# Pair attention of a one-core transformer tower: exponentials over three PSUM banks, two units in flight, a ring of six steps

## The chip, the cores and the metric

The kernel runs on one core of a Trainium2 chip. Times are device microseconds (us) of one execution. PE is TensorE, DVE is VectorE, ACT is ScalarE, POOL is GpSimd, SP is SyncE. Before: a median of 1665.47 us over 3 runs (1663.53 to 1667.87).

## What is computed

The whole is a tower of eight layers on a state h of 2 batches x 1025 tokens x 64 channels. The change touches one of them, the causal attention of 32 heads that are two channels wide:

```python
def _L2_attn_ref(x, w_qkv, w_proj, qn_w, kn_w):
    B, T, C = x.shape
    HD = 2
    H = C // HD
    qkv = x @ w_qkv.T
    q, k, v = jnp.split(qkv, 3, axis=-1)
    heads = lambda t: t.reshape(B, T, H, HD).transpose(0, 2, 1, 3)
    q = _rmsnorm(heads(q), qn_w)
    k = _rmsnorm(heads(k), kn_w)
    v = heads(v)
    scale = np.float32(1.0 / np.sqrt(HD))
    att = jnp.einsum('bhtd,bhsd->bhts', q, k) * scale
    causal = jnp.tril(jnp.ones((T, T), bool))
    att = jnp.where(causal, att, jnp.float32(-1e30))
    att = jax.nn.softmax(att, axis=-1)
    y = jnp.einsum('bhts,bhsd->bhtd', att, v)
    y = y.transpose(0, 2, 1, 3).reshape(B, T, C)
    return y @ w_proj.T
h = h + _L2_attn_ref(_layernorm(h, axis=-1), L2_attn_w_qkv, L2_attn_w_proj, L2_attn_qn_w, L2_attn_kn_w)
```

For each of 64 pairs of batch and head the kernel takes the exponential of half of a 1024 x 1024 matrix of scores, and the last token apart.

## The kernel before

`program` runs nine stages one after the other, each in blocks that end with a barrier of all engines; `stage_pairs` (L1937) is the sixth. It calls `pairs_prepare` (norms, projections), `pairs_attend` (L2113, the function that the change touches) and `pairs_project`.

`pairs_attend` works on four heads of one batch at a time, 16 such groups (`BH`). A group is cut into nine **steps** (the list `steps`). A step is one block of 128 keys against 512 queries, or two blocks whose queries together make 512: steps 1 and 8 are blocks of 384 and 128 queries, step 2 of 256 and 256. N = 144 steps in all, numbered n; s = n % 9 is the place in the group. A step goes through the engines so:

- **Scores** (PE, L2325): for each of the four heads q a matmul of 12 rows (bf16) x 512 queries into one PSUM bank, the four on rows 0, 32, 64 and 96 of the array. Two heads make a **unit** u, two banks; units use banks 0-1, 2-3, 4-5 in turn, so three are in flight. The first matmul of unit u waits until the exponential of unit u - 3 is done (`exp_ok`, u - 2 of them). The second signals `s_ps`.
- **Exponential** (ACT, L2255): one instruction of 128 x 1024 for each unit, 288 in all, from PSUM into the ring `PT` of RING = 4 steps. It waits for `s_ps`, and from step 4 on at every step for the weighing of step n - 3 (`av_ps`).
- **Mask** (DVE, L2239): for the steps in `diag` (0, 1, 2, 7, 8 of a group) a product with `keep`, 128 x 512, once or (steps 1, 2, 8) twice. It waits for both exponentials of its step.
- **Weighing** (PE, `weigh`, L2291, called by `attend`): weights times values in float32, four heads on the four column groups of the array, accumulated in bank 6. Half 0 of the queries ends with step 2, half 1 with step 8; DVE then copies bank 6 into `Yc` (L2232), and the next half waits for that copy (`y_sb`). The second block of step 2 is weighed with step 3, so step 2 has 256 columns, step 3 has 512 + 256.
- **Turns** (`TURNS`, PE L2280 and L2271 by way of bank 7, brought out by DVE at L2197 or L2185/L2187): after steps 0 to 3 of a group two transposes of the next group's q and two of its k, after steps 4 to 6 the results `Yc` of the group before.

What fixes the order is PE's own program, written out in the loop over n: the scores of step n, the weighing of step n - 2, the turn of step n. Every engine takes its instructions in that order and waits at the head of its queue. DVE's loop at step n is: the copy of bank 6 if the weighing of n - 2 ended a half, the turn, the mask of step n.

```python
for n in range(N + per):
    ...
        attend(n - 2)
    for t in turns_at(n):
        turn(*t)
```

Of the kernel before, what the change touches and what calls it, by code (L numbers as in the profile page):

```python
# [14 lines left out]
ACT = mybir.ActivationFunctionType  # L15
# [2097 lines left out]
def pairs_attend(nc, K, A, Q12, K12, V1, qk, Yt, YL):  # L2113


    SCALE = float(np.float32(1.0 / np.sqrt(2)))
# [6 lines left out]
    steps += [[(1, 5, 0, 128, 384), (1, 7, 384, 384, 128)]]  # L2123
    per = len(steps)
    diag = {0: (0,), 1: (0, 384), 2: (0, 256), 7: (0,), 8: (0, 384)}
    RING = 4
    N = BH * per

    TURNS = {0: ("q", 0), 1: ("q", 1), 2: ("k", 0), 3: ("k", 1), 4: ("y", 0), 5: ("y", 1), 6: ("y", 2)}
# [17 lines left out]
    masked = [0]  # L2147
    for n in range(N):
        masked.append(masked[-1] + (n % per in diag))
    with ExitStack() as ctx:  # L2150
        sb = lambda n, s, dt=F32: K.sb("pt_" + n, s, dt, ctx=ctx)
        sem = lambda n: K.sem("pt_" + n)
        ps = K.ps
# [1 line left out]
        keep = sb("keep", [128, 128])  # L2155
        QT = sb("QT", [128, 2, 1024], BF16)
        KT = sb("KT", [128, 2, 1024], BF16)
        PT = sb("PT", [128, RING, 4, 512])
        Yc = sb("Yc", [128, 2, 1024])
        rec = sb("rec", [128, 3, 4])  # L2160
        LP = sb("LP", [128, 2, 9, 96])
# [6 lines left out]
        with nc.Block() as block:  # L2168
# [4 lines left out]
            @block.vector  # L2173
            def _(dve):
                link = Chain(dve, chain)
                tt = nc.vector.tensor_tensor
                nc.vector.tensor_copy(identb[:], K.ident[:]).then_inc(id_ok, 1)

                def bring(bh, which, i):
                    dve.wait_ge(turn_ps, number[bh, which, i] + 1)  # L2180
                    if which == "y":
                        t0, t1 = YTILES[i]
                        y = ps[:, 7, 0:128 * (t1 - t0)].rearrange("p (t h e) -> p t h e", h=4, e=32)
                        r = rec[:, 0:t1 - t0]
                        link(nc.vector.reciprocal(r, y[:, :, :, 2]))  # L2185
                        g = 4 * (bh % 8)
                        ins = tt(Yt[:, (bh // 8) * 8 + t0:(bh // 8) * 8 + t1, g:g + 4], y[:, :, :, 0:2],  # L2187
                                 r.unsqueeze(3).to_broadcast([128, t1 - t0, 4, 2]), ALU.mult)
                    elif which == "last":
                        y = ps[0:1, 7, 0:192].rearrange("p (b h e) -> p b h e", b=2, e=3)  # L2190
                        link(nc.vector.reciprocal(LR[:], y[:, :, :, 2]))
                        ins = tt(YL[:], y[:, :, :, 0:2], LR[:].unsqueeze(3).to_broadcast([1, 2, 32, 2]), ALU.mult)
                    else:
                        if bh >= 2:
                            dve.wait_ge(s_ps, 2 * per * (bh - 1))
                        dst = QT if which == "q" else KT
                        ins = nc.vector.tensor_copy(dst[:, bh % 2, 512 * i:512 * i + 512],  # L2197
                                                    ps[:, 7, :].bitcast(BF16)[:, 0:512])
                    ins.then_inc(turn_sb, 1)

                def last_scores(b):
                    q = qk[:, 16 + b, 0:64]
                    kk = LP[:, b, :, 0:64]
                    link(tt(kk[:, 0:8], qk[:, 8 * b:8 * b + 8, 64:128], bc(q, 8), ALU.mult))
                    link(tt(kk[:, 8], qk[:, 16 + b, 64:128], q, ALU.mult))
                    ins = nc.vector.tensor_reduce(LS[:, b], kk.rearrange("p t (h e) -> p t h e", e=2), AX.X, ALU.add)
                    ins.then_inc(ls_ok, 1)

                def last_weights(b):
                    if b == 0:  # L2210
                        dve.wait_ge(le_ok, 1)
                        link(nc.vector.tensor_scalar(LS[:, :, 8], LS[:, :, 8], K.ident[:, 0:1], None, ALU.mult))
                    w = LP[:, b].rearrange("p t (h e) -> p t h e", e=3)
                    v = V1[:, 8 * b:8 * b + 8, 0:96].rearrange("p t (h e) -> p t h e", e=3)
                    link(tt(w[:, 0:8], v, LS[:, b, 0:8].unsqueeze(3).to_broadcast([128, 8, 32, 3]), ALU.mult))
                    link(tt(w[:, 8], V1[:, 16 + b, 0:96].rearrange("p (h e) -> p h e", e=3), bcl(LS[:, b, 8], 3),
                            ALU.mult))
                    nc.vector.tensor_reduce(LW[:, b], LP[:, b].rearrange("p t c -> p c t"), AX.X,
                                            ALU.add).then_inc(lw_ok, 1)

                for t in FIRST:
                    bring(*t)
                dve.wait_ge(c_in, 16)
                for n in range(N + per):
                    bh, s = n // per, n % per
                    if n >= 2 and n - 2 < N and (n - 2) % per in (2, 8):
                        c = (n - 2) % per // 8
                        k = 2 * ((n - 2) // per) + c
                        dve.wait_ge(av_ps, n - 1)
                        if k >= 4:  # L2230
                            dve.wait_ge(turn_ps, number[k // 2 - 2, "y", 2] + 1)
                        nc.vector.tensor_copy(Yc[:, k // 2 % 2, 512 * c:512 * c + 512], ps[:, 6, :]).then_inc(y_sb, 1)  # L2232
                    for t in turns_at(n):
                        bring(*t)
                    if n < N and s in diag:
                        dve.wait_ge(exp_ok, 2 * n + 2)
                        for c0 in diag[s]:
                            d = PT[:, n % RING, :, c0:c0 + 128]
                            ins = tt(d, d, bc(keep[:], 4), ALU.mult)  # L2239
                        ins.then_inc(mask_ok, 1)  # L2240
                    if s == 5 and bh in (1, 2):
                        last_scores(bh - 1)
                    if s == 5 and bh in (3, 4):
                        last_weights(bh - 3)

            @block.scalar
            def _(act):
                for n in range(N):
                    if n >= 4:
                        act.wait_ge(av_ps, n - 2)  # L2250
                    for i in range(2):
                        u = 2 * n + i
                        act.wait_ge(s_ps, u + 1)
                        b0 = 2 * (u % 3)
                        nc.scalar.activation(PT[:, n % RING, 2 * i:2 * i + 2, :], ps[:, b0:b0 + 2, :], ACT.Exp,  # L2255
                                             scale=SCALE).then_inc(exp_ok, 1)
                    if n == 3 * per:
                        act.wait_ge(ls_ok, 2)
                        nc.scalar.activation(LS[:], LS[:], ACT.Exp, scale=SCALE).then_inc(le_ok, 1)

            @block.tensor
            def _(pe):
# [23 lines left out]
                def weigh(n, parts, start, stop):  # L2286
                    bh = n // per
                    for k, (c, j, p0, q0, w) in enumerate(parts):
                        for q in range(4):
                            v0 = 3 * (4 * (bh % 8) + q)  # L2290
                            ins = nc.tensor.matmul(ps[32 * q:32 * q + 32, 6, q0:q0 + w],  # L2291
                                                   V1[:, (bh // 8) * 8 + j, v0:v0 + 32],
                                                   PT[:, n % RING, q, p0:p0 + w], start=start and k == 0,
                                                   stop=stop and k == len(parts) - 1, skip_group_check=True)
                    return ins

                def attend(n):
                    bh, s = n // per, n % per
                    pe.wait_ge(exp_ok, 2 * n + 2)
                    if s in diag:  # L2300
                        pe.wait_ge(mask_ok, masked[n + 1])
                    if s in (0, 3) and n:
# [12 lines left out]
                for n in range(N + per):  # L2315
                    bh, s = n // per, n % per
                    if n < N:
                        if s == 0:
                            pe.wait_ge(turn_sb, number[bh, "k", 1] + 1)
                        for q in range(4):  # L2320
                            u = 2 * n + q // 2
                            if q % 2 == 0 and u >= 3:
                                pe.wait_ge(exp_ok, u - 2)
                            for c, j, p0, q0, w in steps[s]:
                                ins = nc.tensor.matmul(ps[:, 2 * (u % 3) + q % 2, p0:p0 + w],  # L2325
                                                       KT[32 * q:32 * q + 12, bh % 2, j * 128:(j + 1) * 128],
                                                       QT[32 * q:32 * q + 12, bh % 2, c * 512 + q0:c * 512 + q0 + w],
                                                       start=True, stop=True)
                            if q % 2:
                                ins.then_inc(s_ps, 1)  # L2330
                    if 2 <= n < N + 2:
                        attend(n - 2)
# [718 lines left out]
```

## Time and profile before

| | |
|---|---|
| median of 3 runs | 1665.47 us |
| profiled execution, its own time | 1676.74 us |
| its span on the core | 1675.0 us |
| busy: PE, DVE, ACT, POOL | 1342.4, 1018.7, 861.0, 367.5 us |
| TensorE clock granted, share of full speed, whole span | 0.83 |
| `pairs_attend`: first exponential starts, last ends | 786.7 us, 1055.3 us |
| exponentials of the stage (L2255) | 288, 266.1 us busy |

Busy shares are of the whole span and average over stages; the stage in question is some 270 us of it, and what bounds it is to be read from a stretch within it. A waiting instruction is named with what released it. Matmuls overlap one another: a row that says "x8 ... 1.07" is eight matmuls from the start of the first to the end of the last, and PE can start the next kind before that end.

### The profile page before, as it was taken

The numbers are of one execution on the slowest core, as the hardware profiler recorded it, in microseconds if no ns is written. First come the engines' busy times: TensorE is split into PE (matmuls) and PEld (weight loads), VectorE is DVE, ScalarE is ACT, GpSimd is POOL, SyncE is SP. The second block draws the span as 40 slices with busy tenths as digits, with TensorE's granted clock in tenths as the row PEclk, the third lists the DMA queues.
The fourth block names the chain that finished last, engine by engine and source line by source line (L and its number), as shares of the span: only waits on it lengthen the run. The fifth ranks groups of instructions, "written<-read, shape, count | busy, mean of one in ns | idle before, by whom it ended". The sixth has DMA issues, their size and how long they took to land. (4 is left out here: it accounts for less than half of the span.)

```text
span 1675.0 us, 28770 instructions
## 1 busy us (share of the span) xinstructions
PE 1342.4 (80%) x11573; PEld 780.8 (47%) x11573; DVE 1018.7 (61%) x1983; ACT 861.0 (51%) x1716; POOL 367.5 (22%) x409
## 2 busy tenths in 40 slices
PE   6658993975488929973999999686899999977995
PEld 3547982775434425541333333444454445554342
DVE  0467556845794185657574545425799999964233
ACT  1330222121304723346999999321799999952121
POOL 0002400000051200000000000000599999940000
PEclk9865996555656959985999999767699999996898
DMA  6000000013000000000000000001000000001000
GB/s 124 8 12 10 1 2 8 1 22 49 11 1 1 1 14 1 1 2 2 1 2 1 2 1 2 10 0 23 9 2 2 2 2 2 2 5 25 1 1 13
DMA packets 37692, 15.87 MB, mean 9 GB/s; under 512 B 33588, under 2 KB 36798, under 8 KB 37296
## 3 DMA queue, kind: packets, MB, share of 16 engines
q1 hardware_dynamic: 37560, 14.04, 4.1%
q8 instruction: 92, 1.51, 0.4%
q14 instruction: 40, 0.33, 0.1%
HBM read 12.98 MB, written 1.05 MB: 8 GB/s over the span
## 5 line engine op out<-in xcount | busy, mean ns | idle before, releaser
L2910 POOL TENSOR_SCALAR da_AD<-di_QH,di_KH 128x256 f32<-128x256 f32 x320 | 287.5, 926 | 52.8 <-POOLq L2689 47.4
L2895 ACT ACTIVATE da_AD<-ps,di_NK 128x256 f32<-128x256 f32 x760 | 288.3, 840 | 0.5
L2871 DVE TENSOR_TENSOR da_AD<-ps,di_KH 128x1024 f32<-128x1024 f32 x240 | 273.4, 1216 | 0.9
L2255 ACT ACTIVATE pt_PT<-ps 128x1024 f32<-128x1024 f32 x288 | 266.1, 1103 | 6.3 <-PE ps L2325 6.0
L2946 PE MATMUL ps<-da_AD,da_win 128*32 128x256 f32 x4080 | 241.7, 384 | 19.6 <-ACT da_AD L2895 14.6
L2946 PEld LDWEIGHTS ps<-da_AD,da_win 128*32 128x32 f32 x4080 | 123.0, 110 | 133.9 <-ACT da_AD L2895 39.5
L2291 PE MATMUL ps<-pt_PT,pa_V 128*32 128x512 f32 (+3 forms) x1536 | 155.5, 499 | 8.3 <-DVE pt_Yc L2232 3.2
L2239 DVE TENSOR_TENSOR pt_PT<-pt_PT,pt_keep 128x512 f32<-128x512 f32 x128 | 84.2, 689 | 61.2 <-ACT pt_PT L2255 60.1
L2325 PE MATMUL ps<-pt_QT,pt_KT 12*128 12x512 bf16 (+3 forms) x768 | 80.1, 334 | 3.2 <-DVE pt_KT L2197 0.5
L2623 PE MATMUL ps<-cp_XT,cp_W 96*128 96x342 f32 x192 | 75.1, 518 | 0.0
L2568 ACT ACTIVATE cp_H<-ps 128x342 f32<-128x342 f32 x48 | 21.9, 457 | 102.8 <-PE ps L2623 102.8
L2449 POOL MEMSET sw_xo<- 114x576 f32 x1 | 0.6, 578 | 330.3 <-POOLq L151 330.3
L1923 PE MATMUL ps<-mt_X,ew_wp 128*128 128x342 bf16 (+1 forms) x396 | 70.2, 314 | 1.3 <-ACT mt_WT L1854 0.8
L2291 PEld LDWEIGHTS ps<-pt_PT,pa_V 128*32 128x32 f32 x1536 | 38.9, 109 | 64.8 <-issue 63.6
L2535 DVE TENSOR_SCALAR cp_H<-ps 128x342 f32<-128x342 f32 x48 | 24.2, 513 | 72.5 <-PE ps L2623 72.4
L1868 ACT ACTIVATE mt_act<-ps 128x342 f32<-128x342 f32 (+1 forms) x66 | 30.1, 456 | 69.5 <-PE ps L1925 66.1
L662 ACT COPY rc_T<-ps 114x228 f32<-114x228 f32 x54 | 18.9, 349 | 81.7 <-PE ps L609 81.7
L1835 DVE TENSOR_TENSOR mt_prod<-ps,mt_act 128x342 f32<-128x342 f32 (+1 forms) x66 | 33.9, 514 | 37.3 <-ACT mt_act L1868 37.3
L2623 PEld LDWEIGHTS ps<-cp_XT,cp_W 96*128 96x128 f32 x192 | 35.8, 207 | 36.7 <-issue 28.4
L1582 PE MATMUL ps<-gq_KT,gq_QT 96*114 96x342 bf16 (+2 forms) x144 | 44.1, 433 | 10.7 <-DVE gm_mx L1511 8.6
L1923 PEld LDWEIGHTS ps<-mt_X,ew_wp 128*128 128x128 bf16 (+1 forms) x396 | 36.2, 101 | 34.6 <-DVE mt_H L1836 14.3
L654 DVE TENSOR_TENSOR rc_XX<-ps,rc_XX 114x456 f32<-114x456 f32 (+1 forms) x54 | 32.1, 594 | 32.1 <-PE ps L623 32.1
(721 smaller groups left out, 2391.3 us busy)
## 6 DMA issues: line engine op xcount, KB each, us to landing
em_xs<-in_x_dram SPq DMA_DIRECT2D x2, 1152.0 KB, 14.0
em_xs<-in_x_dram SPq DMA_DIRECT2D x2, 1024.0 KB, 18.2
ew_win<-in_L_ffn_w_dram SPq DMA_DIRECT2D x4, 320.0 KB
cp_W<-in_L_ffn_w_dram SPq DMA_DIRECT2D x2, 512.0 KB
em_WS<-in_L_tok_W_dram SPq DMA_DIRECT2D x8, 72.0 KB
la_blk<-la_scratch SPq DMA_DIRECT2D x8, 64.1 KB
dp_tokrow<-in_c_tokenrow_dram SPq DMA_DIRECT2D x1, 513.0 KB
la_scratch<-la_q SPq DMA_DIRECT2D x1, 512.0 KB
```

The lines of the kernel that those rows point to most:

```text
L1582: ins = nc.tensor.matmul(ps[0:P, b0 + c, 0:w], QT[0:96, h, t * P:(t + 1) * P], KT[0:96, h // 2, k0:k0 + w], start=True, stop=True)
L1835: link(tt(prod[0:r, n % 2], ps[0:r, b0 + 1, 0:GRP], act_sb[0:r, n % 2], ALU.mult))
L1923: nc.tensor.matmul(ps[0:r, b0 + i, 0:GRP], wp[:, k, i, 128 * c:128 * c + r], x_[:, cols], start=(k == 0), stop=(k == 2))
L2239: ins = tt(d, d, bc(keep[:], 4), ALU.mult)
L2255: nc.scalar.activation(PT[:, n % RING, 2 * i:2 * i + 2, :], ps[:, b0:b0 + 2, :], ACT.Exp, scale=SCALE).then_inc(exp_ok, 1)
L2291: ins = nc.tensor.matmul(ps[32 * q:32 * q + 32, 6, q0:q0 + w], V1[:, (bh // 8) * 8 + j, v0:v0 + 32], PT[:, n % RING, q, p0:p0 + w], start= ...
L2325: ins = nc.tensor.matmul(ps[:, 2 * (u % 3) + q % 2, p0:p0 + w], KT[32 * q:32 * q + 12, bh % 2, j * 128:(j + 1) * 128], QT[32 * q:32 * q + ...
L2623: nc.tensor.matmul(ps[:, n % 4, 0:GRP], W1[:, c * 128:(c + 1) * 128], XT[:, g * GRP:(g + 1) * GRP], start=True, stop=True).then_inc(up_ps, 1)
L2871: nc.vector.tensor_tensor(AD[:, n % RING], bc(QD[:, u % 2], 4), bcl(kk, SELP), ALU.max).then_inc(ad_dve, 1)
L2895: ins = nc.scalar.activation(AD[:, n % RING, q], QA[:, u % 2], ACT.Abs, bias=NK[:, u, s:s + 1])
L2910: ins = nc.gpsimd.tensor_scalar(AD[:, n % RING, q], QH[:, u], KH[:, u, s:s + 1], None, ALU.max)
L2946: ins = nc.tensor.matmul(ps[32 * q:32 * q + 32, e % 4, 0:SELP], w, AD[:, n % RING, q], start=False, stop=last, skip_group_check=True)
```

## The change

`WIDE` = 3 heads make a unit instead of two. A unit is three consecutive score banks of the stream m = 4n + q, so that a unit crosses steps: in three steps (12 heads) lie four units, [q0 q1 q2], [q3 | q0 q1], [q2 q3 | q0], [q1 q2 q3]. Units use banks 0-2 and 3-5 in turn, so two are in flight: the first matmul of unit u waits for the exponential of unit u - 2. The exponential is one instruction of 128 x 1536, 192 in all. The ring of weights `PT` becomes 24 slots, six steps. Masks and weighings of step n wait for `units(n)`, the last unit that holds a head of step n.

```diff
-    RING = 4
+    RING = 6
+    WIDE = 3
+    SLOTS = 4 * RING
...
+    def units(n):
+        return (4 * n + 3) // WIDE + 1
...
-        PT = sb("PT", [128, RING, 4, 512])
+        PT = sb("PT", [128, SLOTS, 512])
...
-                        dve.wait_ge(exp_ok, 2 * n + 2)
+                        dve.wait_ge(exp_ok, units(n))
...
-                for n in range(N):
-                    if n >= 4:
-                        act.wait_ge(av_ps, n - 2)
-                    for i in range(2):
-                        u = 2 * n + i
-                        act.wait_ge(s_ps, u + 1)
-                        b0 = 2 * (u % 3)
-                        nc.scalar.activation(PT[:, n % RING, 2 * i:2 * i + 2, :], ps[:, b0:b0 + 2, :], ACT.Exp,
-                                             scale=SCALE).then_inc(exp_ok, 1)
+                for u in range(4 * N // WIDE):
+                    last = WIDE * u + WIDE - 1
+                    if last >= SLOTS:
+                        act.wait_ge(av_ps, (last - SLOTS) // 4 + 2)
+                    act.wait_ge(s_ps, u + 1)
+                    b0, p0 = WIDE * (u % 2), WIDE * u % SLOTS
+                    nc.scalar.activation(PT[:, p0:p0 + WIDE, :], ps[:, b0:b0 + WIDE, :], ACT.Exp,
+                                         scale=SCALE).then_inc(exp_ok, 1)
...
                         for q in range(4):
-                            u = 2 * n + q // 2
-                            if q % 2 == 0 and u >= 3:
-                                pe.wait_ge(exp_ok, u - 2)
+                            m = 4 * n + q
+                            if m % WIDE == 0 and m >= 2 * WIDE:
+                                pe.wait_ge(exp_ok, m // WIDE - 1)
...
-                                ins = nc.tensor.matmul(ps[:, 2 * (u % 3) + q % 2, p0:p0 + w],
+                                ins = nc.tensor.matmul(ps[:, m % (2 * WIDE), p0:p0 + w],
...
-                            if q % 2:
+                            if m % WIDE == WIDE - 1:
                                 ins.then_inc(s_ps, 1)
```

The matmuls of PE keep their order; what moves is where it waits for an exponential, and after which matmul it signals one. The lists below give PE's instructions with the semaphores waited for. The program reuses semaphores of earlier stages, so they have those names: `md_hid_sb` is `exp_ok`, `md_y_ps` is `mask_ok`, `md_row_sb` is `turn_sb`, `la_c_in` is `y_sb`, `md_y_sb` is `av_ps`. L2325 is the scores (L2330 after the change), L2291 (L2296) the weighing, L2271 (L2276) and L2280 (L2285) turns.

**PE, steps 6 and 7 of the second group, before.**

```order
L2325 MATMUL ps<-pt_QT,pt_KT 128x512 [waits md_hid_sb]
L2325 MATMUL ps<-pt_QT,pt_KT 128x512
L2325 MATMUL ps<-pt_QT,pt_KT 128x512 [waits md_hid_sb]
L2325 MATMUL ps<-pt_QT,pt_KT 128x512
L2291 MATMUL ps<-pt_PT,pa_V 32x512 [waits md_hid_sb]
L2291 MATMUL ps<-pt_PT,pa_V 32x512 x3
L2271 MATMUL ps<-ident,pt_Yc 128x128 [waits la_c_in,md_row_sb]
L2271 MATMUL ps<-ident,pt_Yc 128x128
L2325 MATMUL ps<-pt_QT,pt_KT 128x512 [waits md_hid_sb]
L2325 MATMUL ps<-pt_QT,pt_KT 128x512
L2325 MATMUL ps<-pt_QT,pt_KT 128x512 [waits md_hid_sb]
L2325 MATMUL ps<-pt_QT,pt_KT 128x512
```

**The same place after the change.**

```order
L2330 MATMUL ps<-pt_QT,pt_KT 128x512 [waits md_hid_sb]
L2330 MATMUL ps<-pt_QT,pt_KT 128x512 x2
L2330 MATMUL ps<-pt_QT,pt_KT 128x512 [waits md_hid_sb]
L2296 MATMUL ps<-pt_PT,pa_V 32x512 [waits md_hid_sb]
L2296 MATMUL ps<-pt_PT,pa_V 32x512 x3
L2276 MATMUL ps<-ident,pt_Yc 128x128 [waits la_c_in,md_row_sb]
L2276 MATMUL ps<-ident,pt_Yc 128x128
L2330 MATMUL ps<-pt_QT,pt_KT 128x512 x2
L2330 MATMUL ps<-pt_QT,pt_KT 128x512 [waits md_hid_sb]
L2330 MATMUL ps<-pt_QT,pt_KT 128x512
L2296 MATMUL ps<-pt_PT,pa_V 32x512 [waits md_hid_sb]
```

Before, a unit's two score matmuls stand side by side. After, the unit that begins with the second wait has its first matmul ahead of the weighing and the turn, and its other two behind them; the next one has two ahead of a weighing and one behind.

**PE, steps 0 and 1 of the third group, before.**

```order
L2325 MATMUL ps<-pt_QT,pt_KT 128x512 [waits md_hid_sb,md_row_sb]
L2325 MATMUL ps<-pt_QT,pt_KT 128x512
L2325 MATMUL ps<-pt_QT,pt_KT 128x512 [waits md_hid_sb]
L2325 MATMUL ps<-pt_QT,pt_KT 128x512
L2291 MATMUL ps<-pt_PT,pa_V 32x512 [waits md_y_ps,md_hid_sb]
L2291 MATMUL ps<-pt_PT,pa_V 32x512 x3
L2280 MATMUL ps<-pt_identb,pa_Q 128x128 [waits md_row_sb]
L2280 MATMUL ps<-pt_identb,pa_Q 128x128 x3
L2325 MATMUL ps<-pt_QT,pt_KT 128x384 [waits md_hid_sb]
```

**The same place after the change.**

```order
L2330 MATMUL ps<-pt_QT,pt_KT 128x512 [waits md_hid_sb,md_row_sb]
L2330 MATMUL ps<-pt_QT,pt_KT 128x512 x2
L2330 MATMUL ps<-pt_QT,pt_KT 128x512 [waits md_hid_sb]
L2296 MATMUL ps<-pt_PT,pa_V 32x512 [waits md_y_ps,md_hid_sb]
L2296 MATMUL ps<-pt_PT,pa_V 32x512 x3
L2285 MATMUL ps<-pt_identb,pa_Q 128x128 [waits md_row_sb]
L2285 MATMUL ps<-pt_identb,pa_Q 128x128 x3
L2330 MATMUL ps<-pt_QT,pt_KT 128x384
L2330 MATMUL ps<-pt_QT,pt_KT 128x128
L2330 MATMUL ps<-pt_QT,pt_KT 128x384
L2330 MATMUL ps<-pt_QT,pt_KT 128x128
L2330 MATMUL ps<-pt_QT,pt_KT 128x384 [waits md_hid_sb]
```

Here the weighing and a turn of four transposes have come between the first matmul of the second unit and its other heads.

**DVE, steps 0 and 1 of a group, after the change (the order of before, with other line numbers).** L2203 brings a turn out, L2245 is the mask, L2238 the copy of bank 6; `md_row_ps` is `turn_ps`, `md_hid_ps` is `s_ps`.

```order
L2203 COPY pt_QT<-ps 128x512 [waits md_hid_ps,md_row_ps]
L2245 TENSOR_TENSOR pt_PT<-pt_PT,pt_keep 128x4x128 [waits md_hid_sb]
L2238 COPY pt_Yc<-ps 128x512 [waits md_row_ps,md_y_sb]
L2203 COPY pt_QT<-ps 128x512 [waits md_hid_ps,md_row_ps]
L2245 TENSOR_TENSOR pt_PT<-pt_PT,pt_keep 128x4x128 [waits md_hid_sb]
L2245 TENSOR_TENSOR pt_PT<-pt_PT,pt_keep 128x4x128
```

The mask of step 0 stands ahead of the copy of bank 6 (step 8 of the group before). That order is not new; what the mask waits for is: the unit that also holds two heads of step 1.

## Rows read from the trace of the kernel before

**Rows 1.** Busy time in stretches: start:end, length, busy (x count) of each engine, granted clock, DMA.

```profile
core 0: us, PE busy (x) PEld busy (x) DVE busy (x) ACT busy (x) POOL busy (x), PEclk, DMA share, GB/s
786.00:796.00 10.00, 9.73 (x72) 3.15 (x76) 4.75 (x10) 7.54 (x8) 0.00 (x0) 0.52 0.01 2
796.00:1061.00 265.00, 252.44 (x2606) 85.72 (x2602) 149.34 (x323) 258.93 (x281) 0.00 (x0) 1.00 0.01 1
...
277.00:402.00 125.00, 102.02 (x412) 88.52 (x413) 70.49 (x178) 26.57 (x51) 2.51 (x5) 0.50 0.08 12
536.00:590.00 54.00, 46.72 (x406) 21.65 (x402) 9.12 (x22) 37.20 (x64) 12.86 (x31) 1.00 0.03 7
```

**Rows 2.** Groups of ACT by form: busy us, mean ns of one, idle before.

```profile
L2895 ACT ACTIVATE da_AD<-ps,di_NK 128x256 f32<-128x256 f32 x760 | 288.3, 840 | 0.5
L2255 ACT ACTIVATE pt_PT<-ps 128x1024 f32<-128x1024 f32 x288 | 266.1, 1103 | 6.3 <-PE ps L2325 6.0
L1665 ACT ACTIVATE gt_PT<-ps 114x684 f32<-114x684 f32 x48 | 32.8, 738 | 10.6 <-PE ps L1706 10.3
...
L1665 ACT ACTIVATE gt_PT<-ps 114x228 f32<-114x228 f32 x12 | 3.7, 359 | 2.9 <-PE ps L1706 2.9
```

**Rows 3.** The exponential's line alone: duration min/median/max in ns, first and last start.

```profile
L2255 ACT ACTIVATE pt_PT<-ps x288: 1017/1105/1217, 786.7 to 1054.2; 128x1024 f32<-128x1024 f32 x144
```

**Rows 4.** PE in order of time, 896 to 909 us: start, us, what.

```profile
895.99 0.64 PE L2291 MATMUL ps<-pt_PT,pa_V 128*32 128x256 f32 x8
896.57 0.55 PE L2271 MATMUL ps<-ident,pt_Yc 128*128 128x128 f32 x3
...
897.05 0.67 PE L2325 MATMUL ps<-pt_QT,pt_KT 12*128 12x512 bf16 x4
897.64 1.50 PE L2291 MATMUL ps<-pt_PT,pa_V 128*32 128x512 f32 x16
899.07 0.55 PE L2271 MATMUL ps<-ident,pt_Yc 128*128 128x128 f32 x3
899.55 0.40 PE L2325 MATMUL ps<-pt_QT,pt_KT 12*128 12x512 bf16 x4
899.88 1.07 PE L2291 MATMUL ps<-pt_PT,pa_V 128*32 128x512 f32 x8
900.88 0.44 PE L2271 MATMUL ps<-ident,pt_Yc 128*128 128x128 f32 x2
901.25 0.39 PE L2325 MATMUL ps<-pt_QT,pt_KT 12*128 12x512 bf16 x4
901.57 1.07 PE L2291 MATMUL ps<-pt_PT,pa_V 128*32 128x512 f32 x8
902.57 0.78 PE L2325 MATMUL ps<-pt_QT,pt_KT 12*128 12x384 bf16 x8
...
907.12 1.07 PE L2291 MATMUL ps<-pt_PT,pa_V 128*32 128x384 f32 x16
908.12 0.40 PE L2280 MATMUL ps<-pt_identb,pa_Q 128*128 128x128 bf16 x4
908.45 0.41 PE L2325 MATMUL ps<-pt_QT,pt_KT 12*128 12x256 bf16 x8
```

**Rows 5.** ACT by windows around 900 us; PEld's load released by an exponential's end.

```profile
894.28 2.99 ACT L2255 ACTIVATE pt_PT<-ps 128x1024 f32<-128x1024 f32 x3
...
894.28 5.74 ACT L2255 ACTIVATE pt_PT<-ps 128x1024 f32<-128x1024 f32 x6
...
897.32 0.09 PEld L2325 LDWEIGHTS ps<-pt_QT,pt_KT 12*128 12x128 bf16 x2 [0.19 <-ACT pt_PT L2255]
898.82 7.75 ACT L2255 ACTIVATE pt_PT<-ps 128x1024 f32<-128x1024 f32 x8
900.04 1.02 ACT L2255 ACTIVATE pt_PT<-ps 128x1024 f32<-128x1024 f32 x1
```

**Rows 6.** DVE masks and copies of bank 6 by form; between them, a weighing after a copy.

```profile
L2239 DVE TENSOR_TENSOR pt_PT<-pt_PT,pt_keep 128x512 f32<-128x512 f32 x128 | 84.2, 689 | 61.2 <-ACT pt_PT L2255 60.1
...
909.08 0.64 PE L2291 MATMUL ps<-pt_PT,pa_V 128*32 128x512 f32 x4 [0.23 <-DVE pt_Yc L2232]
L2232 DVE COPY pt_Yc<-ps 128x512 f32<-128x512 f32 x32 | 22.1, 692 | 10.4 <-PE ps L2291 9.7
```

**Rows 7.** Waits in 786 to 1058 us: us in total, times, longest.

```profile
PEld ps L2325 <- ACT pt_PT L2255: 35.3, 89, 0.8
...
ACT pt_PT L2255 <- PE ps L2325: 6.0, 3, 4.2
```

**Rows 8.** PE at the stage's start, at the lower clock.

```profile
790.19 1.94 PE L2291 MATMUL ps<-pt_PT,pa_V 128*32 128x512 f32 x8
792.05 0.61 PE L2280 MATMUL ps<-pt_identb,pa_K 128*128 128x128 bf16 x4
792.60 0.61 PE L2325 MATMUL ps<-pt_QT,pt_KT 12*128 12x512 bf16 x4
```

More of the change, by code:

```diff
@@ L2194, in bring @@
                         if bh >= 2:
-                            dve.wait_ge(s_ps, 2 * per * (bh - 1))
+                            dve.wait_ge(s_ps, 4 * per * (bh - 1) // WIDE)
                         dst = QT if which == "q" else KT
@@ L2235, in _ @@
                     if n < N and s in diag:
-                        dve.wait_ge(exp_ok, 2 * n + 2)
+                        dve.wait_ge(exp_ok, units(n))
                         for c0 in diag[s]:
-                            d = PT[:, n % RING, :, c0:c0 + 128]
+                            d = PT[:, 4 * n % SLOTS:4 * n % SLOTS + 4, c0:c0 + 128]
                             ins = tt(d, d, bc(keep[:], 4), ALU.mult)
@@ L2247, in _ @@
             def _(act):
-                for n in range(N):
-                    if n >= 4:
-                        act.wait_ge(av_ps, n - 2)
-                    for i in range(2):
-                        u = 2 * n + i
-                        act.wait_ge(s_ps, u + 1)
-                        b0 = 2 * (u % 3)
-                        nc.scalar.activation(PT[:, n % RING, 2 * i:2 * i + 2, :], ps[:, b0:b0 + 2, :], ACT.Exp,
-                                             scale=SCALE).then_inc(exp_ok, 1)
-                    if n == 3 * per:
+                for u in range(4 * N // WIDE):
[6 more added lines that the diff above has]
+                                         scale=SCALE).then_inc(exp_ok, 1)
+                    if u == 3 * 4 * per // WIDE:
                         act.wait_ge(ls_ok, 2)
@@ L2292, in weigh @@
                                                    V1[:, (bh // 8) * 8 + j, v0:v0 + 32],
-                                                   PT[:, n % RING, q, p0:p0 + w], start=start and k == 0,
+                                                   PT[:, (4 * n + q) % SLOTS, p0:p0 + w], start=start and k == 0,
                                                    stop=stop and k == len(parts) - 1, skip_group_check=True)
@@ L2298, in attend @@
                     bh, s = n // per, n % per
-                    pe.wait_ge(exp_ok, 2 * n + 2)
+                    pe.wait_ge(exp_ok, units(n))
                     if s in diag:
```

## The prediction

> **What bounds the kernel now.** I read the busy time in stretches first. The change lies in one stage, which starts at 786 us. In its steady part ACT is busy 258.93 us of 265, and the clock granted to PE is 1.00 [rows 1]. Next the groups: ACT's part is 288 exponentials, 266.1 us busy with 6.3 us idle [rows 2]. So ACT sets the stage's time: 266.1 / 16 = 16.63 us for each group of four heads (18 exponentials of 0.924). The waits agree: PE waited 89 times for an exponential, ACT only 3 times for scores [rows 7].
>
> PE in order of time shows how near it comes [rows 4]. I take the distance from the start of one kind to the start of the next: scores 0.33 (899.55 to 899.88), weighing of 512 columns 1.00 (901.57 to 902.57), of 384 + 128 also 1.00 (907.12 to 908.12), of 256 0.58 (895.99 to 896.57), of 512 + 256 1.43 (897.64 to 899.07), turn of three 0.48, of two 0.37, of q or k 0.33 (908.12 to 908.45). A group has nine scores (2.97), weighings of nine times 512 columns (9.0) and seven turns (2.65): 14.6, some 15 with the scores in two pieces. PE has 1.6 us to spare in 16.6.
>
> The same rows show what happens when a long piece of PE lies between an exponential's end and the next scores. The exponentials from 894.28 end at 897.27; PE loads weights at 897.32 [rows 5] and from 897.33 does the last two scores of a step, the long weighing, a turn of three, and at 899.55 new scores, which end at 899.95 [rows 4]. ACT starts on them at 900.04. In a stream it starts one every 0.91 (898.82 is the sixth from 894.28), so it was due at 899.73 [rows 5]. ACT has lost 0.31 us there, with three units in flight; as exponentials overlap, only 0.02 of it show as idle. From it I take three delays: exponential's end to scores 0.06, scores' start to their end 0.40, that to ACT's start 0.09 (0.49 together).
>
> **What the change costs, part by part.** *The exponential of 1536.* Alone, 228 columns take 359 ns, 684 take 738 and 1024 take 1017 [rows 2, 3]: 0.83 ns a column. So 1536 take L = 1.44 us alone. In a stream 1024 start every 0.91 us; 0.42 more makes E = 1.33. Lower bound: the 256-wide ones take 288.3 / 760 = 0.379 each in a stream, against 0.924, or 0.71 ns a column: E = 1.29, L = 1.38. I take the first, from exponentials of the same kind. Twelve units a group by 1.33 are 15.97 against 16.63: ACT needs 0.66 less, 10.5 us in the stage. That is the whole gain there is, if ACT never waits. The Trainium skill, "ScalarE: Activation LUTs", section "What ACT_TABLE_LOAD costs", gives 186 ns + 0.833 ns a column, with 93 ns of overlap back to back; by it the 96 instructions removed would be worth 96 x 93 ns = 8.9 us, an estimate. The rows give 18 x 0.907 less 15.97, or 0.06 for each of the six removed in a group, and the 0.31 on top.
>
> *Two units in flight, cut across the steps.* A unit may be written once the unit two before it is done. Two of four units have a weighing in the middle. Let ACT start unit U3 of the last cycle at T, with its end at T + 1.44, and take weighings w1, w2 and turns t1, t2. U0 starts at T + 1.33. PE writes the first bank of U1 at T + 1.50 (0.33), weighs w1, turns t1, writes two banks (0.49): U1 starts at T + 2.32 + w1 + t1 (T + 3.32 + t1 for a weighing of 1.00), where ACT was free at T + 2.66. For U2 PE goes on: 0.33, w2, t2, one bank and 0.49. U2 starts at T + 2.65 + w1 + w2 + t1 + t2, or 1.33 after U1. U3 and the next U0 are whole, and follow by 1.33 each if nothing else is late. Three steps so take 5.98 + t1 + t2, against 5.44 of ACT before.
>
> Through a group, measured from the start of its U0:
> - Steps 0 to 2: U1 after 2.33 (t1 = 0.33), U2 after 1.75 (t2 = 0.33, pieces of 384 and 128 about 0.1), U3 after 1.33. The next U0 is late by DVE: the mask of step 0 now waits for U1's end (0.05, 0.69), the copy of bank 6 stands behind it (0.69) and the weighing of step 0 waits for that copy [rows 6]; then 1.00, a turn 0.33, scores 0.49. U0 starts 1.44 + 3.31 after U1: at 7.08.
> - Steps 3 to 5: mask of step 1 and turn let U1 come 1.97 later, then 1.37 (weighing 0.58, turn 0.48), 1.33, and 1.51 for U0, behind the weighing of 1.43 and a turn of 0.48: 6.19.
> - Steps 6 to 8: 2.16 (turn 0.37), 1.36, 1.33, 1.33: 6.18.
>
> Sum 19.45 us against 16.63: 2.82 a group, 45.1 in 16. The first group has no results to turn nor copy to wait for, about 1 less: **+44 us**. The lower clock at the start (0.52 for 10 us [rows 1]) is there in both, and may cost up to 2 more where PE is now in the path.
>
> *Ring of six.* ACT's wait for a weighing moves from three steps back to five. I cost it at nothing: the 0.31 before 900.04 is explained by scores that ended at 899.95, while the weighing ended at 899.14 (897.64 + 1.50) [rows 4]. Masks and weighings are the same in number. The masks' 84.2 us of DVE lie beside; what they hold up is counted above.
>
> **The sum.** The profiled execution took 1676.74 us, 11.3 above the median; nothing in the stage explains that, so I carry the difference over: 1720.7 for it, 1665.47 + 44 = **1709.5** for the median. Bounds: with E = 1.29 and L = 1.38, 0.27 less a group, 1705. Exponentials in a stream last longer, up to 1217 ns with a median of 1105 [rows 3]; 0.09 more of L enters about four times a group, and gives 1715. Twelve distances of PE and DVE a group, each good to 0.05, are 10 us either way. Own range 1698 to 1722.
>
> **Rivals.**
> - *The change works: PE always has three banks ready, ACT is the bound.* 15.97 a group, 1665.5 - 10.5 = **1655**. For it: PE busy for 15 of 16. It needs w1 + t1 under 0.34, where U1 is no longer late (T + 2.32 + w1 + t1 against T + 2.66); the weighing alone is 1.00 [rows 4], and the same reckoning gives 900.04 for the late exponential of before. 0.07.
> - *Half of the stalls vanish,* in distances that overlap where I add them: each group 1.4 less or more so, down to no change at **1665**: 0.03.
> - *PE's clock falls.* PE is now idle in many short waits; 15 of 19.45 us is 77% of the time. The trace has both: a stretch at 1.00 with PE busy 46.72 of 54, and one at 0.50 with 102.02 of 125 [rows 1]. At the lower level a weighing of 512 takes 1.86 (790.19 to 792.05) and a turn 0.55 [rows 8]: nine weighings 16.7, seven turns 3.9, nine scores at about a turn 5.0, together 25.6, over 6 us a group more. In half of the stage that is 50 us, **1759**; from the first fall it decides. The Trainium skill, "TensorE: Matmul & The Clock Gate", section "A second HAM failure mode: psum-queue depth-cycling", says that a PE which idles briefly again and again while it cycles through PSUM banks swings between its two clocks. By that page the later time would come; no stretch of this stage shows it so far, at 95% busy. 0.09.
>
> **How the numbers follow.** My forecast has 0.81. A measurement of this kernel can tell about 0.3% (5 us) from no change. Faster by more: only the first rival, 0.07. Same: 0.03. Slower: forecast and clock, 0.90. The range needs 8 in 10: nine tenths of the forecast's 0.81 in its own range, and a little more on both sides for stalls partly absorbed and for a clock that falls a short while: 1694 to 1728.
>
> **What would show it.** Exponentials: 192, of about 1.44 to 1.5 us each. From the first one's start to the last one's, 267.4 us before, some 311. ACT idle before them, released by the scores: 16 x (19.45 - 15.97) = 56 us, in gaps up to 1.0 (the largest at steps 0 to 1, then 7 and 4). PE waits less for exponentials than it does now and still is in ACT's path. Clock 1.00 after the first 10 us. If gaps are there only where a turn lies inside the unit, the turns and not the weighings decide; if ACT's idle is under 15 us, the forecast is wrong and the first rival right; if the weighings' distances grow to 1.86, it is the clock; a mean far from 1.44 means the exponential was mis-sized.

## The result, and the profile after

The changed kernel takes 1732.76 us (median of 4 runs, 1723.87 to 1737.02), against 1664.50 for the kernel before (4 runs, 1657.42 to 1667.87): a ratio of 1.0413, 95% interval 1.0366 to 1.0459. It is slower, as forecast, by 68 us and not by 44, and outside the range.

One profile below, that with two full-array matmuls, is of a disturbed execution (1759.32 us) and is read for this stage alone; the medians given are of all runs of a kernel, the ratios leave such executions out.

The first figures to compare are those of ACT. Groups of the stage by form, as [rows 2], of the changed kernel:

```profile
L2260 ACT ACTIVATE pt_PT<-ps 128x1536 f32<-128x1536 f32 x192 | 268.7, 1452 | 81.5 <-PE ps L2330 80.8
L2296 PE MATMUL ps<-pt_PT,pa_V 128*32 128x512 f32 x768 | 118.2, 691 | 9.3 <-DVE pt_Yc L2238 7.7 <-DVE pt_PT L2245 1.2
```

The exponentials are 96 fewer and ACT is as busy as before, 268.7 us (rows now count each alone, since few overlap). Its idle time has gone from 6.3 to 81.5 us, and the scores end nearly all of it. The line alone, as [rows 3]:

```profile
L2260 ACT ACTIVATE pt_PT<-ps x192: 1445/1450/1479, 782.1 to 1127.2; 128x1536 f32<-128x1536 f32 x192
```

The stage, from the first exponential to the end of the last, has grown from 268.6 to 346.5 us, 78 more; the stages behind it took 16 less in this execution, at a granted clock of 0.90 instead of 0.87, and those ahead 5 less. The stretches, as [rows 1]:

```profile
core 0: us, PE busy (x) PEld busy (x) DVE busy (x) ACT busy (x) POOL busy (x), PEclk, DMA share, GB/s
796.00:810.00 14.00, 11.55 (x124) 3.54 (x124) 6.86 (x12) 11.85 (x9) 0.00 (x0) 1.00 0.01 2
843.00:901.00 58.00, 51.06 (x506) 17.00 (x506) 33.50 (x69) 50.72 (x38) 0.00 (x0) 1.00 0.01 1
961.00:1105.00 144.00, 134.07 (x1008) 38.69 (x1008) 54.61 (x121) 101.03 (x74) 0.00 (x0) 0.71 0.00 1
```

So there are two kinds of groups. Measured from each group's first exponential to the next group's (every twelfth), they take 19.57, 19.46, 22.08, 19.46 three times, 20.75, 19.46 twice, and then six of 23.90 to 23.97; the last group, from its first start to its last end, takes 23.86. ACT in order of time, one of the first kind, from 862.72 on:

```profile
862.72 1.48 ACT L2260 ACTIVATE pt_PT<-ps 128x1536 f32<-128x1536 f32 x1
865.04 1.45 ACT L2260 ACTIVATE pt_PT<-ps 128x1536 f32<-128x1536 f32 x1 [0.85 <-PE ps L2330]
866.70 2.80 ACT L2260 ACTIVATE pt_PT<-ps 128x1536 f32<-128x1536 f32 x2 [0.20 <-PE ps L2330]
869.79 1.45 ACT L2260 ACTIVATE pt_PT<-ps 128x1536 f32<-128x1536 f32 x1 [0.30 <-PE ps L2330]
871.69 5.68 ACT L2260 ACTIVATE pt_PT<-ps 128x1536 f32<-128x1536 f32 x4 [0.45 <-PE ps L2330]
878.17 5.48 ACT L2260 ACTIVATE pt_PT<-ps 128x1536 f32<-128x1536 f32 x4 [0.80 <-PE ps L2330]
884.50 1.45 ACT L2260 ACTIVATE pt_PT<-ps 128x1536 f32<-128x1536 f32 x1 [0.86 <-PE ps L2330]
```

The gaps stand at the cut units, as the working said: 2.33 us from the first start to the second, 1.66 to the third. A pair in a stream takes 2.80, one alone 1.45, so E is 1.35 and L 1.45. PE in order of time shows what lies in the cut, and where DVE comes in:

```profile
862.90 0.38 PE L2330 MATMUL ps<-pt_QT,pt_KT 12*128 12x512 bf16 x1 [0.86 <-ACT pt_PT L2260]
863.21 1.07 PE L2296 MATMUL ps<-pt_PT,pa_V 128*32 128x512 f32 x8
864.21 0.40 PE L2285 MATMUL ps<-pt_identb,pa_Q 128*128 128x128 bf16 x4
864.54 0.41 PE L2330 MATMUL ps<-pt_QT,pt_KT 12*128 12x384 bf16 x8
...
866.52 0.69 DVE L2245 TENSOR_TENSOR pt_PT<-pt_PT,pt_keep 128x512 f32<-128x512 f32 x1 [1.45 <-ACT pt_PT L2260]
867.13 0.68 DVE L2238 COPY pt_Yc<-ps 128x512 f32<-128x512 f32 x1
867.96 1.07 PE L2296 MATMUL ps<-pt_PT,pa_V 128*32 128x512 f32 x8 [1.02 <-DVE pt_Yc L2238]
```

One score matmul, then 1.33 us of weighing and turn, then the rest of the unit; mask, copy and weighing one behind the other. A late group has the same order at the clock's lower level, first ACT, then PE one group before:

```profile
1009.21 1.47 ACT L2260 ACTIVATE pt_PT<-ps 128x1536 f32<-128x1536 f32 x1
1013.05 1.45 ACT L2260 ACTIVATE pt_PT<-ps 128x1536 f32<-128x1536 f32 x1 [2.37 <-PE ps L2330]
1015.99 2.79 ACT L2260 ACTIVATE pt_PT<-ps 128x1536 f32<-128x1536 f32 x2 [1.49 <-PE ps L2330]
```

```profile
986.00 1.94 PE L2296 MATMUL ps<-pt_PT,pa_V 128*32 128x512 f32 x8
987.86 0.61 PE L2285 MATMUL ps<-pt_identb,pa_Q 128*128 128x128 bf16 x4
988.40 0.62 PE L2330 MATMUL ps<-pt_QT,pt_KT 12*128 12x384 bf16 x8
```

The weighing takes 1.86 to the next start, the figure of [rows 8], and the cut unit comes 3.84 us after the one before instead of 2.33. The clock is low for a part of each late group and full again for the rest:

```profile
1009.20:1022.90 13.70, 13.45 (x97) 3.90 (x97) 6.60 (x12) 7.59 (x7) 0.00 (x0) 0.50 0.00 1
1022.90:1033.10 10.20, 8.89 (x79) 2.55 (x71) 2.50 (x8) 9.15 (x7) 0.00 (x0) 1.00 0.01 2
```

### The profile page after: what moved, and what is told of

It is laid out like the page before. It is cut to its first block and busy times, and to the rows that moved or that the text cites. A ratio compares the mean times of both kernels' runs of the same rounds, so it can differ in the third digit from the quotient of the medians.

```text
span 1732.2 us, 28718 instructions
## 1 busy us (share of the span) xinstructions
PE 1373.9 (79%) x11573; PEld 780.4 (45%) x11573; DVE 1018.4 (59%) x1983; ACT 862.1 (50%) x1620; POOL 366.5 (21%) x409
## 5 line engine op out<-in xcount | busy, mean ns | idle before, releaser
L2260 ACT ACTIVATE pt_PT<-ps 128x1536 f32<-128x1536 f32 x192 | 268.7, 1452 | 81.5 <-PE ps L2330 80.8
L2296 PE MATMUL ps<-pt_PT,pa_V 128*32 128x512 f32 (+3 forms) x1536 | 186.0, 587 | 10.2 <-DVE pt_Yc L2238 7.7
L2245 DVE TENSOR_TENSOR pt_PT<-pt_PT,pt_keep 128x512 f32<-128x512 f32 x128 | 84.1, 688 | 95.9 <-ACT pt_PT L2260 95.7
L2330 PE MATMUL ps<-pt_QT,pt_KT 12*128 12x512 bf16 (+3 forms) x768 | 99.2, 375 | 25.5 <-ACT pt_PT L2260 23.5
L2296 PEld LDWEIGHTS ps<-pt_PT,pa_V 128*32 128x32 f32 x1536 | 40.0, 122 | 83.3 <-issue 81.4
L2330 PEld LDWEIGHTS ps<-pt_QT,pt_KT 12*128 12x128 bf16 x768 | 25.2, 94 | 98.1 <-ACT pt_PT L2260 50.1
L2628 PE MATMUL ps<-cp_XT,cp_W 96*128 96x342 f32 x192 | 68.6, 481 | 0.0
## 6 DMA issues: line engine op xcount, KB each, us to landing
em_xs<-in_x_dram SPq DMA_DIRECT2D x2, 1152.0 KB, 13.7
```

The lines of the kernel that those rows point to most:

```text
L2260: nc.scalar.activation(PT[:, p0:p0 + WIDE, :], ps[:, b0:b0 + WIDE, :], ACT.Exp, scale=SCALE).then_inc(exp_ok, 1)
L2330: ins = nc.tensor.matmul(ps[:, m % (2 * WIDE), p0:p0 + w], KT[32 * q:32 * q + 12, bh % 2, j * 128:(j + 1) * 128], QT[32 * q:32 * q + 12, b ...
L2628: nc.tensor.matmul(ps[:, n % 4, 0:GRP], W1[:, c * 128:(c + 1) * 128], XT[:, g * GRP:(g + 1) * GRP], start=True, stop=True).then_inc(up_ps, 1)
```

## The experiments

Theory: three things add up. Two units in flight leave too little room, the cuts put a weighing into that room, and the changed stream of work lets TensorE's clock fall. Each of the following takes one of these alone. "Before" is run on the same chip beside each.

**The ring alone.**

```diff
-    RING = 4
+    RING = 6
...
-                    if n >= 4:
-                        act.wait_ge(av_ps, n - 2)
+                    if n >= 6:
+                        act.wait_ge(av_ps, n - 4)
```

> The kernel before with the ring of weights at six steps and nothing else. Theory (scores, not the ring, are what ACT waits for once a group): no change, 1664 us, the late exponential once a group still there, 192-fold pattern of the change absent, 288 exponentials from first to last start in 267 us. Rival (the weighing of three steps back held ACT up once a group, 0.31 us x 16): 5 us faster, 1659 us.

1663.81 us, ratio 0.9981 (0.9950 to 1.0012). Groups of 16.63 as before, the late exponential still there. The ring is worth nothing to the kernel before. It is a condition of the change: the slots must divide by three, which those of a ring of four don't.

**Two units in flight, not cut.**

```diff
-                            if q % 2 == 0 and u >= 3:
-                                pe.wait_ge(exp_ok, u - 2)
+                            if q % 2 == 0 and u >= 2:
+                                pe.wait_ge(exp_ok, u - 1)
...
-                        b0 = 2 * (u % 3)
+                        b0 = 2 * (u % 2)
```

> The kernel before (units of two banks, exponentials of 1024) with two units in flight instead of three: the scores of unit u wait for the exponential of unit u - 2. Theory (depth is a cost of its own): by the delays read before the change, 18.75 us a group at the full clock against 16.63, so 34 us more, 1698 us; more, up to 1730 us, if TensorE's clock falls in the stage as it did in the changed kernel from 961 us on. Rival (only units that are cut by a weighing cost anything, depth is free): 1664 us.

1695.11 us, ratio 1.0196 (1.0131 to 1.0262). Groups of 18.65, the exponentials at their old size. Depth costs 2.0 us a group by itself, at a clock of 0.99 from 810 to 1080 us. Its group of ACT:

```profile
L2255 ACT ACTIVATE pt_PT<-ps 128x1024 f32<-128x1024 f32 x288 | 273.2, 1025 | 34.5 <-PE ps L2325 32.7
```

**Units of three banks, two in flight, not cut.** PE's loop runs over units and puts a weighing and a turn after the second, third and fourth of four:

```diff
-                for n in range(N + per):
...
+                for v in range(4 * (N + per) // 3):
+                    for m in range(3 * v, 3 * v + 3):
...
+                    if v % 4:
+                        n = 3 * (v // 4) + v % 4 - 1
+                        if 2 <= n < N + 2:
+                            attend(n - 2)
+                        for t in turns_at(n):
+                            turn(*t)
```

> The changed kernel with PE's order written by units: the three scores of a unit side by side, and a weighing with its turn after the second, third and fourth unit of each three steps. Exponentials of 1536, two in flight and the ring of six stay. Theory (the cut units are the loss): 17.06 us a group, stage of about 273 us, 7 us over before, 1671 us, clock 1.00 throughout. Rival (two units in flight are the loss, wherever the weighings stand): near the changed kernel, 19 to 20 us a group, 1710 us or more.

1679.21 us (10 runs, 1668.39 to 1705.82), ratio 1.0069 (1.0017 to 1.0121). Groups of 17.24: 2.2 us a group, 35 us, came from the cuts, that is from the order of PE's program. Twelve exponentials at 1.33 would be 16.0; the rest is two late starts in each group, DVE, PE and ACT in order of time:

```profile
930.83 0.69 DVE L2245 TENSOR_TENSOR pt_PT<-pt_PT,pt_keep 128x512 f32<-128x512 f32 x1 [0.48 <-ACT pt_PT L2260]
931.44 0.68 DVE L2238 COPY pt_Yc<-ps 128x512 f32<-128x512 f32 x1
932.27 1.07 PE L2296 MATMUL ps<-pt_PT,pa_V 128*32 128x512 f32 x8 [0.38 <-ACT pt_PT L2260]
933.60 0.60 PE L2331 MATMUL ps<-pt_QT,pt_KT 12*128 12x512 bf16 x6
934.10 5.48 ACT L2260 ACTIVATE pt_PT<-ps 128x1536 f32<-128x1536 f32 x4 [0.61 <-PE ps L2331]
...
937.47 1.50 PE L2296 MATMUL ps<-pt_PT,pa_V 128*32 128x512 f32 x16
938.90 0.55 PE L2276 MATMUL ps<-ident,pt_Yc 128*128 128x128 f32 x3
939.38 0.65 PE L2331 MATMUL ps<-pt_QT,pt_KT 12*128 12x512 bf16 x6
939.88 1.45 ACT L2260 ACTIVATE pt_PT<-ps 128x1536 f32<-128x1536 f32 x1 [0.30 <-PE ps L2331]
```

The first, 0.61 us, is the link through DVE: mask, then the copy of bank 6, which ends at 932.12, then the weighing that waits for it. (The profile names ACT as the releaser, whose exponential ended 0.02 later; the weighing follows the copy's end by the same 0.15 in every group here.) The second, 0.30 us, is the long weighing and a turn of three ahead of the scores, the late exponential of the kernel before.

**Is it PE's idle time that brings the clock down?** The changed kernel, with the scores of whole units written three times:

```diff
-                            for c, j, p0, q0, w in steps[s]:
+                            for c, j, p0, q0, w in steps[s] * (3 if m // WIDE % 4 in (0, 3) else 1):
```

> The changed kernel with the score matmuls of its whole units (first and fourth of four) given three times over, the same numbers into the same banks; more work for PE where it has time to spare. Theory (PE's idle time brings its clock down, and the low clock is 4.5 us a group in half of the changed kernel's groups): the clock stays at 1.00 through the stage, a group takes 20.1 us everywhere, the stage 323 us against 347, so 24 us faster than the changed kernel, 1709 us. Rival (the fall of the clock has another cause, work alone counts): groups of 20.1 us and others of 24.6, 10 us slower than the changed kernel, 1743 us.

1749.57 us, ratio 1.0515 (1.0446 to 1.0583). The rival was right in that the clock fell all the same: groups of 20.3 at the full clock, two of 28.3, one of 25. Its stretches:

```profile
960.00:982.00 22.00, 21.88 (x240) 8.36 (x236) 9.64 (x21) 18.81 (x14) 0.00 (x0) 1.00 0.01 2
984.00:1002.00 18.00, 18.00 (x135) 6.13 (x131) 6.59 (x14) 9.61 (x8) 0.00 (x0) 0.50 0.00 1
```

PE was busy for 21.88 of 22 us, and then the clock fell. Idle time as the rows show it is not the condition. The added matmuls use 12 of 128 rows.

**The same with matmuls over all 128 rows.** Two of 512 columns, or one, before the scores of each whole unit, into the bank that these overwrite:

```diff
+                            if m % WIDE == 0 and m // WIDE % 4 in (0, 3):
+                                for _ in range(2):
+                                    nc.tensor.matmul(ps[:, m % (2 * WIDE), :], KT[:, bh % 2, 0:128],
+                                                     QT[:, bh % 2, 0:512], start=True, stop=True)
```

> The changed kernel with two more matmuls (all 128 rows, 128 columns of weights, 512 wide, bf16) ahead of the scores of each whole unit, written to the bank that the scores then overwrite. The time added is that of the scores given thrice, some 20.3 us a group at the full clock. Theory (the clock follows work on the whole array, which matmuls of 12 rows are not): clock 1.00 through the steady part, groups of 20.3 us, stage 325 us, 1712 us, 37 us under the scores given thrice. Rival (the clock falls for another reason than too little work): falls as with the scores given thrice, 1745 us.

1728.55 us, ratio 1.0357 (1.0285 to 1.0429). The stage did as the theory says: clock 1.00, groups of 20.37 to the end, 326.5 us in all. The time is 9 us or more above the 1712 expected in each run; the stage is not where that lies.

> The changed kernel with one such full-array matmul (0.21 us) instead of two ahead of the scores of each whole unit. Theory (the clock follows work on the whole array; the waits give 19.7 us a group with this filler): if the one is enough, clock 1.00, all groups 19.7 us, stage 312 us, 1712 to 1718 us, less than the changed kernel although it does more; if it is not, some groups near 24. Rival (filler only shifts the falls by chance): as many low groups as in the changed kernel, 1735 us.

1711.99 us (1701.32 to 1721.96), ratio 1.0254 (1.0170 to 1.0338). Groups of 19.72, against 19.7 worked out, and the stage 315.7 us instead of 346.5:

```profile
810.00:1090.00 280.00, 262.08 (x2473) 86.33 (x2467) 139.18 (x298) 241.14 (x172) 0.00 (x0) 1.00 0.01 1
```

A kernel that does more is 20 us faster than the changed one, and near the 1709.5 that was forecast for the full clock.

**The changed kernel once more**, nothing edited.

> The changed kernel once more. Theory (the full-clock group is fixed at 19.46 us by the waits, and only the number of groups at the lower clock varies): groups of 19.46 again wherever the clock is 1.00, the time 1733 us, give or take 10, by the number of low groups. Rival (the low groups are a one-off): all groups 19.46, 1709 us.

1732.04 us, ratio 1.0400 (1.0340 to 1.0460). Groups of 19.46 and of 23.9 again, but in other places: three low ones early, six of 19.46 (four of them in a row), others of 20.9 and 22.1. The waits are the same in each execution, the low groups are not. The stage took 334.5 us here, and its last group, at the full clock, 18.93.

**The other way round: the kernel before with less weighing.**

```diff
+                    elif s in (4, 5, 6):
+                        ins = weigh(n, [(1, s - 3, 0, 0, 128)], False, False)
```

> The kernel before with the weighings of steps 4, 5 and 6 of each group cut to 128 of their 512 columns (part of the sums is left out), everything else as it was. ACT stays the bound, 16.3 us a group, and PE does a quarter less of weighing. Theory (too little work on the whole array brings the clock down, whatever the units): the clock falls in the stage; while it is low PE needs over 20 us a group, so stage and time grow, 1690 us or more. Rival (the falls belong to the changed kernel's pattern of waits): clock 1.00, no group over 16.7 us, 1660 us.

1695.51 us, ratio 1.0175 (1.0116 to 1.0234). Taking a quarter of the weighing away (part of the sums is left out, here and in the next two kernels) made it 29 us slower. The clock was 0.83 in the stage, groups 17.6 to 20.1. PE in order of time, over a fall:

```profile
964.79 0.43 PE L2291 MATMUL ps<-pt_PT,pa_V 128*32 128x128 f32 x8
...
966.63 0.43 PE L2291 MATMUL ps<-pt_PT,pa_V 128*32 128x128 f32 x8
967.31 0.39 PE L2327 MATMUL ps<-pt_QT,pt_KT 12*128 12x512 bf16 x2 [0.25 <-ACT pt_PT L2255]
968.13 0.43 PE L2327 MATMUL ps<-pt_QT,pt_KT 12*128 12x512 bf16 x2 [0.44 <-ACT pt_PT L2255]
968.50 1.93 PE L2291 MATMUL ps<-pt_PT,pa_V 128*32 128x512 f32 x8
970.36 0.61 PE L2280 MATMUL ps<-pt_identb,pa_Q 128*128 128x128 bf16 x4
```

After the light weighings the next full one runs at the lower clock, 1.93 us instead of 1.07. Filler against this, first in the wrong place and then in the right one:

```diff
+                            if q % 2 == 0 and s in (4, 5, 6):
+                                for _ in range(2 - q // 2):
+                                    nc.tensor.matmul(ps[:, 2 * (u % 3), :], KT[:, bh % 2, 0:128],
+                                                     QT[:, bh % 2, 0:512], start=True, stop=True)
```

> The kernel with the light weighing (steps 4 to 6 cut to 128 columns, part of the sums left out), and in the same steps full-array matmuls of 0.21 us ahead of the scores, two before the first unit and one before the second, 1.9 us a group, as much PE time as the weighing lost; the scores overwrite what they write. Theory: the clock is back at 1.00, groups of 16.3 to 16.7 us, 1664 us, 30 us faster than without the filler. Rival (the shorter weighings themselves, not the missing work, upset the order): 1695 us or more.

1729.46 us, ratio 1.0322 (1.0229 to 1.0415), the theory's forecast missed by 65 us. The filler stood by the scores of steps 4 to 6, but PE weighs two steps later; the clock fell in every group, after the steps without filler. The whole stage, and around one fall, which comes just behind light weighings at 968.14 and 969.19:

```profile
810.00:1100.00 290.00, 275.76 (x2519) 92.82 (x2512) 138.82 (x298) 242.83 (x257) 0.00 (x0) 0.84 0.01 1
957.00:970.70 13.70, 12.90 (x131) 4.85 (x129) 6.12 (x15) 11.07 (x13) 0.00 (x0) 1.00 0.01 2
970.70:977.50 6.80, 6.63 (x52) 1.70 (x48) 3.01 (x5) 5.83 (x7) 0.00 (x0) 0.50 0.01 2
```

With `s in (6, 7, 8)` instead:

> As the light weighing with filler, but the filler ahead of the scores of steps 6, 7 and 8, where PE runs the weighings that were cut (it weighs two steps back); part of the sums is left out as there. Theory (the clock follows full-array work over a short stretch, so the filler must stand where the weighing is missing): clock 1.00, groups of 16.3 to 16.8 us, 1664 to 1670 us. Rival (filler of this kind does not stand in for float32 weighing): falls in every group, 1690 us or more.

1683.60 us, ratio 1.0105 (1.0066 to 1.0143), and no fall:

```profile
796.00:1050.00 254.00, 247.33 (x2579) 93.04 (x2578) 141.10 (x302) 245.11 (x265) 0.00 (x0) 1.00 0.01 1
```

The clock is as the theory says, the time is not: groups of 17.38, not 16.3 to 16.8. Here the filler lies on ACT's path: ACT waits for scores 28 times between 796 and 1050 us, 8.9 us in all. Still 12 us faster than the same kernel without it.

**Whole units with the clock held**, one such matmul before the second unit of four (`if m % WIDE == 0 and v % 4 == 1`).

> The order by whole units with one full-array matmul (0.21 us) ahead of the scores of the second unit of each four. Theory (whole units cost 0.6 us a group against before by their waits alone, the rest of their spread is the clock): clock 1.00, groups of 17.3 to 17.5 us, 1676 us, runs closer together. Rival (the waits are not it, and with the clock held they vanish): 1664 us.

1677.63 us (1673.78 to 1680.52), ratio 1.0083 (1.0057 to 1.0108). Clock 1.00, groups of 17.72, 0.2 over the upper end of what was expected. So exponentials of 1536 with two in flight are about 14 us slower than before even uncut and at the full clock, of which 8 us are the filler (17.72 against 17.24, 16 groups).

**An attempt to gain on before:** the turns of the results one step later.

```diff
-    TURNS = {0: ("q", 0), 1: ("q", 1), 2: ("k", 0), 3: ("k", 1), 4: ("y", 0), 5: ("y", 1), 6: ("y", 2)}
+    TURNS = {0: ("q", 0), 1: ("q", 1), 2: ("k", 0), 3: ("k", 1), 4: ("y", 0), 6: ("y", 1), 7: ("y", 2)}
```

> The kernel before with the second and third turn of the results one step later (after steps 6 and 7 instead of 5 and 6), so that no turn follows the double weighing. Theory (the lost 0.31 us once a group is the double weighing and a turn of three ahead of the next scores): the late exponential is gone, groups of 16.3 us instead of 16.63, 5 us faster, 1659 us. Rival (ACT would be late there anyway, for the ring or the mask): no change, 1664 us.

1668.09 us, ratio 1.0028 (0.9990 to 1.0065): no difference that can be told. In its trace the loss of 0.31 is gone and two of 0.06 and 0.12 have come at steps 2 and 3, where ACT now arrives early; groups of 16.50 instead of 16.63, the stage 3 us shorter. No version here beats the kernel before.

## Why the prediction was right and wrong

- **What bounds.** Right. ACT set the time before, and after it ACT waits 85 times for scores.
- **Two signs.** Two of those named in "What would show it" came out otherwise. ACT's idle was to be 56 us, 3.5 a group; at the full clock it is 7.3 us in 58 (843 to 901 us), 2.4 a group, since an exponential that starts after a gap keeps ACT busy for 1.45 us where one in a stream adds 1.33, and the working counted the difference as idle. PE was to wait less for exponentials than before; it waits longer, its loads 46.7 us from 786 to 1110 us against 35.3 in the stage before [rows 7]:

```profile
PEld ps L2330 <- ACT pt_PT L2260: 46.7, 81, 1.2
```

- **The exponential.** Right: L 1.45 for 1.44, E 1.35 for 1.33. The Trainium skill's "ScalarE: Activation LUTs", section "What ACT_TABLE_LOAD costs", gives 186 ns and 0.833 ns a column. By it one alone would take 1466 ns, an estimate; the rows have 1445 to 1479.
- **Two in flight, cut.** Right: 19.46 us a group for 19.45, step by step 2.33, 1.66, 1.34, 1.75 against 2.33, 1.75, 1.33, 1.67 in the first four units. That the sum of a group is met to 0.01 is in part luck: single distances are off by up to 0.09 either way (2.25 for 2.16 at steps 6 to 7, 1.66 for 1.75 at steps 0 to 1) and cancel. Two of the parts were tried alone: depth (two units in flight, not cut: 18.65), cuts (19.46 less 17.24). The link through DVE, mask before copy, is seen in the rows, still costs 0.61 us a group in the whole units, and was not tried alone.
- **Ring of six at nothing.** Right: no change in the kernel before, and in the changed kernel scores end 80.8 of ACT's 81.5 us of waiting.
- **The clock.** Here it failed. The sum had nothing for the clock; it stood apart in "PE's clock falls", with 0.09 and a price of 50 us for half of the stage. It came, in both profiles of the changed kernel, and cost 36 us of the stage in the first and 24 in the second. Over 19.46, six groups of the first have 4.4 to 4.5 us, two have 2.6 and 1.3, and the last group has 4.9 over the 18.93 of the second profile. The sign that was named for it, weighings 1.86 apart, is there. The step that failed was to take the stage's record at 95% busy, and a stretch at 1.00 with 46.72 of 54 busy [rows 1], for a sign that the clock would stand it. Three runs show that busy time does not tell: it fell after 21.88 of 22 (scores thrice), and held at 262.08 of 280 (one full-array matmul) and at 247.33 of 254 (filler in its place). The price of a group was nearer: 6 us for one wholly at the lower level, against 4.4 measured with the clock low for 13.7 of 23.9 us.
- **The sum.** Fifteen groups of 19.46 and a last one of 18.93 are 310.8 us, 42 more than the 268.6 of before: the waits, for 44 forecast. The clock's 36 on top make the 78 that the stage shows; in the second profile 42 and 24 make its 66. The whole shows 68 by medians and 57 in the profiled execution, as the stages around it took 21 us less in that one. The code behind the stage is the same in every kernel here, and its time goes with the clock granted there: 599.7 us at 0.90 (two in flight), 603.5 at 0.90 (changed), 618.5 at 0.87 (filler in its place) and 619.7 at 0.87 (before). Why the clock differs there from one execution to the next is open. The range ended at 1728 since the clock's case was left outside it.

For the clock itself: with one or two matmuls over all rows added, and with filler where the weighing was missing, it held; with as much time of 12-row matmuls it did not; it fell when weighing was taken away, and filler two steps early did not help, so the place of the work counts. So what PE does, and where, matters. How much is wanted is not measured here. The Trainium skill, "TensorE: Matmul & The Clock Gate", section "A second HAM failure mode: psum-queue depth-cycling", describes a PE that idles briefly between groups and swings between its clocks; the trace agrees in the swing, from 961 us on in every group. It puts it down to idling, and the kernel with its scores thrice fell without any to be seen.

## What to carry to other kernels

Before making a PSUM unit larger, write down for each unit the longest piece of PE's program between the wait that frees it and its last matmul, and compare it with the time that the units in flight give; larger units that no longer end where the steps end pull other work into that piece. A wider instruction was to save ACT 10 us of its own time here; the waits took that and 42 us more, and 24 to 36 us went on top through TensorE's clock. Where PE has spare time in a stage, treat the full clock as something that a change can lose, with its own chance and price.

## What was not expected

Less work made a kernel slower: 29 us for a quarter less of weighing. More work made it faster: 20 us for one discarded full-array matmul in each whole unit. A PE that is busy all the time, by the rows, can still fall to the lower clock (21.88 of 22 us busy before it, scores thrice).
